# From the experts to the state-space stage: another order of tiles, convolutions and closing, and normalisations applied by ScalarE

## The reference

```python
x = x + _layernorm(attention(_layernorm(x)))      # over the 16 heads of each token
x = x + _layernorm(experts(_layernorm(x)))        # 16 routed experts of 64, top 4, and a shared one of 512
x = x + _layernorm(mamba_block(_layernorm(x)))    # two directions, 512 channels, 16 states
x = x + _layernorm(bitlinear(_layernorm(x)))      # 256 -> 1024 -> 256, relu squared
```

## Time and profile before

| | us |
|---|---|
| median of 3 runs (7385.79 to 7387.61) | 7387.34 |
| the profiled execution | 7389.32 |
| its span, first to last instruction | 7388.0 |
| TensorE busy | 5764.9 (78%) |
| VectorE busy | 5744.5 (78%) |
| GpSimd busy | 4502.9 (61%) |
| ScalarE busy | 3204.9 (43%) |

### The profile page before, as it was taken

The page is one execution under the profiler, slowest core; times in us unless marked ns, Lnnn a source line. Parts: engine busy times, 40 slices in busy tenths (PEclk is TensorE's granted clock), DMA queues, the critical chain, the costliest instruction groups (busy, mean ns, idle before and its releaser), DMA issues. The chain is left out here.

```text
span 7388.0 us, 59778 instructions
## 1 busy us (share of the span) xinstructions
PE 5764.9 (78%) x18532; PEld 3272.5 (44%) x18532; DVE 5744.5 (78%) x6592; ACT 3204.9 (43%) x6391; POOL 4502.9 (61%) x2698
## 2 busy tenths in 40 slices
PE   5778788787787877878778787787877878778887
PEld 4444354343553435534355343544435434454443
DVE  5589964899648995599964998649986599765997
ACT  1166511665116641266412664126641266313763
POOL 3179740897409964199641995419954299443994
PEclk8899998999899998999889998899988999889998
DMA  2011110111101111011110111101111011110111
GB/s 84 17 37 42 36 46 16 40 41 50 30 15 44 41 47 36 15 39 42 45 36 15 40 42 43 44 9 42 42 39 44 12 42 42 40 41 12 45 41 39
DMA packets 238118, 271.64 MB, mean 37 GB/s; under 512 B 144906, under 2 KB 194994, under 8 KB 231860
## 3 DMA queue, kind: packets, MB, share of 16 engines
q1 hardware_dynamic: 237748, 267.25, 11.2%
HBM read 246.13 MB, written 21.07 MB: 36 GB/s over the span
## 5 line engine op out<-in xcount | busy, mean ns | idle before, releaser
L1192 DVE TENSOR_TENSOR_SCAN wk<-ps,wk 128x1024 f32<-128x1024 f32 x1024 | 2316.3, 2275 | 105.4 <-POOL wk L1813 82.0
L1813 POOL TENSOR_TENSOR wk<-wk 128x1024 f32<-128x1024 f32 x1024 | 2380.3, 2360 | 9.2
L1683 ACT ACTIVATE ps<-wk,Aneg 128x255 f32<-128x255 f32 x4096 | 1704.1, 462 | 1218.1 <-DVE wk L1192 1183.8
L1407 PE MATMUL ps<-wk,ident 128*128 128x512 f32 x4096 | 2019.4, 618 | 24.1 <-DVE wk L1212 24.1
L431 POOL TENSOR_SCALAR rstd<-mv 128x4 f32<-128x4 f32 x146 | 36.0, 247 | 2293.4 <-DVE mv L424 2293.4
L1202 DVE TENSOR_TENSOR wk<-wk,ps 128x1024 f32<-128x1024 f32 x856 | 1021.6, 1193 | 14.4 <-PE ps L1402 8.7
L1407 PEld LDWEIGHTS ps<-wk,ident 128*128 128x128 f32 x4096 | 738.1, 197 | 631.7 <-issue 599.4
L1402 PE MATMUL ps<-wk,sel 112*128 112x256 bf16 x856 | 244.4, 286 | 853.1 <-DVE wk L1202 819.3
L537 POOL TENSOR_TENSOR wk<-wk 128x4096 f32<-128x4096 f32 x64 | 529.3, 8275 | 292.9 <-ACT wk L659 292.9
L1402 PEld LDWEIGHTS ps<-wk,sel 112*128 112x128 bf16 x856 | 84.1, 98 | 1153.9 <-DVE wk L1202 1018.1
L1353 PE MATMUL ps<-xnp,inT 128*128 128x256 f32 (+1 forms) x2048 | 561.6, 401 | 33.3 <-DVE wk L1168 13.7
(11 more groups left out here) (187 smaller groups left out, 8039.0 us busy)
## 6 DMA issues: line engine op xcount, KB each, us to landing
wk<-bc_scr SPq DMA_DIRECT2D x256, 512.0 KB, 3.6
wk<-bc_scr SPq DMA_DIRECT2D x56, 384.0 KB, 3.4
wk<-in_wgT SPq DMA_DIRECT2D x8, 1536.0 KB, 6.6
wk<-in_wuT SPq DMA_DIRECT2D x8, 1536.0 KB, 9.6
wk<-in_wdn SPq DMA_DIRECT2D x8, 1536.0 KB, 6.3
wk<-in_x SPq DMA_DIRECT2D x18, 512.0 KB, 4.0
o_scr<-wk SPq DMA_DIRECT2D x64, 128.0 KB, 3.0
wk<-o_scr SPq DMA_DIRECT2D x32, 256.0 KB, 3.4
```

Of the source, the lines that this page charges most:

```text
L1192: V.tensor_tensor_scan(h, in_time(d, flat(decay(m))), h, 0.0, ALU.mult, ALU.add).then_inc(scanned, 1)
L1407: mm = nc.tensor.matmul(bank(j), ident[:], h[:, 2 * j:2 * j + 2, :] .rearrange("p e t -> p (e t)"), start=first, stop=last)
L1683: nc.scalar.activation(decay(m)[:, e, rest(d)], dl[g % 2][:, e, rest(d)], ACT.Exp, scale=Aneg[:, d, e, n:n + 1]).then_inc(dA_done, 1)
L1813: nc.gpsimd.tensor_tensor(hb[n], du[g % 2], col(Bb[j % 2][:, n % NB, :]) .broadcast_to([P, NDI, MC]), ALU.mult).then_inc(dbu, 1)
```

## The change

`FIRST` becomes: X of unit 0, XD and LG of unit 0, X of unit 1. TensorE's order is X(0) four times, tile 4, XD, LG, LG, tile 5, two X(1), tile 6, two X(1), tile 7. The Z pieces of unit 0 become `GATE`, behind the first row of C, and their copies stand in unit 0 at states 0 to 3. VectorE convolves unit 0, does the softplus operation, then convolves unit 1, and takes the statistics of chunk 1's output before unit 0 and those of the residual sum behind state 1. ScalarE applies both normalisations of chunk 1 (`apply_close`), as an Identity activation with rstd for a scale and `shift` = -mean * rstd for a bias, ahead of the decays of states 0 and 4; GpSimd makes `shift` (`ln_shift`), adds the residual behind state product 1 and makes the second rstd and shift behind state product 2. The transposes of chunk 1 become pieces XE at states 4 to 7 of unit 0 and their copies stand at states 8 to 11; units 2 and 3 wait for them before their first X piece. Places in `wk` move so that `xc` no longer lies under `wdn`.

```diff
-        wdn = area(104 * KB, NJ, C)
+        wdn = area(101 * KB, NJ, C)
...
+        at = 113 * KB
+        inj = [area(at + i * DS * NDI, DS, NDI) for i in range(2)]
...
+        shift = area(at + 2 * MC + DS // 2 * NDI, NT // NCH)
...
+            XE_PE = {4: (0, 0), 5: (1, 0), 6: (0, 1), 7: (1, 1)}
+            XE_ACT = {8: (0, 0), 9: (1, 0), 10: (0, 1), 11: (1, 1)}
...
-            FIRST = (((X, 0, 0), (X, 0, 1)), ((X, 0, 2), (X, 0, 3)), ((X, 1, 0), (X, 1, 1)), ((X, 1, 2), (X, 1, 3)),
-                     ((XD, 0, 0),), ((Z, 0, 0), (Z, 0, 1)), ((LG, 0, 0),), ((LG, 0, 1),),
-                     ((Z, 0, 2), (Z, 0, 3)))
+            FIRST = [(X, 0, e) for e in range(NDI)] + [(XD, 0, 0), (LG, 0, 0), (LG, 0, 1)] + \
+                [(X, 1, e) for e in range(NDI)]
+            GATE = [(Z, 0, e) for e in range(NDI)]
...
-                    for g in range(2):
-                        for e in range(NDI):
-                            conv(g, e)
-                    ln_stats(dve, ecs, ytok, 1, 3, e_ev)
-                    ln_apply(dve, ecs, ytok, 1, 3)
-                    dve.wait_ge(e_added, NT)
-                    ln_stats(dve, ecs, xt, 1, 4)
-                    ln_apply(dve, ecs, xt, 1, 4)
+                    for e in range(NDI):
+                        conv(0, e)
                     softplus(0)
-
-                    dve.wait_ge(e_xn_ready, 3 * KC)
+                    for e in range(NDI):
+                        conv(1, e)
...
+                    ln_stats(dve, ecs, ytok, 1, 3, e_ev)
...
+                            if m == 1:
+                                dve.wait_ge(e_added, NT)
+                                ln_stats(dve, ecs, xt, 1, 4)
...
+                        if kind == X and i == 0 and g in (2, 3):
+                            pe.wait_ge(xe_ev, KC * (g - 1))
...
-                    for n, slot in enumerate(FIRST):
-                        for piece in slot:
+                    for piece in FIRST[0:NDI]:
+                        pre(piece)
+                    down(CT)
+                    for piece in FIRST[NDI:NDI + 3]:
+                        pre(piece)
+                    for n in range(2):
+                        down(CT + 1 + n)
+                        for piece in FIRST[NDI + 3 + 2 * n:NDI + 5 + 2 * n]:
                             pre(piece)
-                        if n < CT:
-                            down(CT + n)
+                    down(NT - 1)
...
-                    xn_tensor(pe, ecs, 1, 4, (0, 2))
-                    pe.wait_ge(e_xn_ready, 3 * KC)
...
                     weights(0)
+                    for piece in GATE:
+                        pre(piece)
...
+                    def apply_close(src, c, nth):
+
+                        act.wait_ge(xe_nb, 2 * (nth - 2))
+                        for i in range(CT):
+                            t = c * CT + i
+                            nc.scalar.activation(ytok[:, t, :], src[:, t, :], ACT.Identity, bias=shift[:, i:i + 1],
+                                                 scale=rstd[:, t:t + 1]).then_inc(ecs[4], 1)
...
+                        if g == 0 and n in XE_ACT:
+                            k, pair = XE_ACT[n]
+                            act.wait_ge(xe_mm, sorted(XE_ACT).index(n) + 1)
+                            at = CH + pair * MC
+                            nc.scalar.copy(xnT[:, k, at:at + MC], pre_slot((XE, k, pair))).then_inc(xe_ev, 1)
...
+                    silu_conv(0)
+                    experts_out(CT)
+                    pre(FIRST[NDI:NDI + 3])
+                    for what in ("abs", "exp"):
+                        soft(0, what)
+                    experts_out(CT + 1)
                     for what in ("ln", "less"):
                         soft(0, what)
-                    xn_scalar(act, ecs, 1, 2, (0, 2))
+                    experts_out(CT + 2)
+                    silu_conv(1)
+                    experts_out(CT + 3)
...
+                            if m == 0:
+                                apply_close(ytok, 1, 3)
+                            if m == 4:
+                                apply_close(xt, 1, 4)
...
+                    def ln_shift(c, nth):
+
+                        rs = rstd[:, c * CT:(c + 1) * CT]
+                        pool.wait_ge(ecs[2], 2 * (nth + 1))
+                        if nth > 3:
+                            pool.wait_ge(ecs[4], nth * CT)
+                        nc.gpsimd.tensor_tensor(shift, mv[:, c * CT:(c + 1) * CT, 0], rs, ALU.mult).then_inc(xe_nb, 1)
+                        pool.wait_ge(xe_nb, 2 * (nth - 3) + 1)
+                        nc.gpsimd.tensor_scalar(shift, shift, -1.0, None, ALU.mult).then_inc(xe_nb, 1)
...
-                    ln_rstd(pool, ecs, 1, 3)
-                    add_residual(pool, ecs, 1, 3)
-                    ln_rstd(pool, ecs, 1, 4)
                     part_c(0)
                     for what in ("lost", "delta", "du"):
                         softplus(0, what)
+                    ln_rstd(pool, ecs, 1, 3)
+                    ln_shift(1, 3)
                     pool.wait_ge(e_ev, NT)
...
+                            if m == 1:
+                                add_residual(pool, ecs, 1, 3)
+                            if m == 2:
+                                ln_rstd(pool, ecs, 1, 4)
+                                ln_shift(1, 4)
```

More of the change, by code:

```diff
@@ L171, in build @@
         hc = [area(at + NDI * MC * i, NDI, MC) for i in range(RC)]
-        inj = [area(at + NDI * MC * RC + i * DS * NDI, DS, NDI) for i in range(2)]
-        at += NDI * MC * RC + 2 * DS * NDI
+        at = 113 * KB
+        inj = [area(at + i * DS * NDI, DS, NDI) for i in range(2)]
+        at += 2 * DS * NDI
         xc = [area(at + i * MC // 2, MC, dt=BF16) for i in range(2)]
@@ L804, in batches @@
                 return NG4 * (g + 1) + max(g, 0)
-            X, Z, XD, LG, OUT, XN = "x", "z", "xd", "lg", "out", "xn"
+            X, Z, XD, LG, OUT, XN, XE = "x", "z", "xd", "lg", "out", "xn", "xe"
             AHEAD = {X: 2, XD: 1, LG: 1, Z: 1}
@@ L821, in pe_piece @@
                     return (XN,) + XN_PE[n]
+                if g == 0 and n in XE_PE:
+                    return (XE,) + XE_PE[n]
                 if n in PRE_PE:
@@ L826, in pe_piece @@
                 return None
-            FIRST = (((X, 0, 0), (X, 0, 1)), ((X, 0, 2), (X, 0, 3)), ((X, 1, 0), (X, 1, 1)), ((X, 1, 2), (X, 1, 3)),
-                     ((XD, 0, 0),), ((Z, 0, 0), (Z, 0, 1)), ((LG, 0, 0),), ((LG, 0, 1),),
-                     ((Z, 0, 2), (Z, 0, 3)))
-            FLAT = [p for slot in FIRST for p in slot]
-            NFIRST = len(FLAT)
-            SLOT = FLAT + [pe_piece(g, n) for g in range(NU) for n in range(DS) if pe_piece(g, n)]
+            FIRST = [(X, 0, e) for e in range(NDI)] + [(XD, 0, 0), (LG, 0, 0), (LG, 0, 1)] + \
+                [(X, 1, e) for e in range(NDI)]
+            GATE = [(Z, 0, e) for e in range(NDI)]
+            NFIRST = len(FIRST)
+            SLOT = FIRST + GATE + [pe_piece(g, n) for g in range(NU) for n in range(DS) if pe_piece(g, n)]
             AT = {p: m for m, p in enumerate(SLOT)}
@@ L856, in build @@
                 "sp_1 sp_ln sp_t sp_c sp_s sp_r sp_sum delta du_done dA_done dbu scanned inj_a inj_e inj_h injected zeroed c_bc "
[L857 removed]
+                "cm sig gated out_mm out_ev xn_mm xn_ev xe_mm xe_ev xe_nb c_part kept pw psig",
                 "x_in0 x_in1 wt_in h_mm relu_done sq_done f_mm f_ev",
@@ L1240, in square @@
                             .then_inc(sq_done, 1)
-                    for g in range(2):
-                        for e in range(NDI):
-                            conv(g, e)
-                    ln_stats(dve, ecs, ytok, 1, 3, e_ev)
-                    ln_apply(dve, ecs, ytok, 1, 3)
-                    dve.wait_ge(e_added, NT)
-                    ln_stats(dve, ecs, xt, 1, 4)
-                    ln_apply(dve, ecs, xt, 1, 4)
+                    for e in range(NDI):
+                        conv(0, e)
                     softplus(0)
-                    dve.wait_ge(e_xn_ready, 3 * KC)
-                    dve.wait_ge(pre_ev, len([p for p in FLAT if p in PLACE]))
+                    for e in range(NDI):
+                        conv(1, e)
+                    dve.wait_ge(pre_ev, len([p for p in FIRST if p in PLACE]))
+                    dve.wait_ge(conv_done, 2 * NDI)
                     for i in range(2):
@@ L1332, in take_slot @@
                             pe.wait_ge(xn_ev, AT[p] - AT[(XN,) + XN_PE[min(XN_PE)]] + 1)
+                        elif p[0] == XE:
+                            pe.wait_ge(xe_ev, AT[p] - AT[(XE,) + XE_PE[min(XE_PE)]] + 1)
                         elif p[0] == X:
@@ L1339, in pre @@
                         kind, g, i = piece
-                        if kind == XN:
+                        if kind in (XN, XE):
                             return ahead_t(piece)
@@ L1387, in ahead_t @@
                         kind, k, pair = piece
-                        pe.wait_ge(mcs[4], 3 * CT)
```

(10 more changed lines are left out.)

2 lines of the change are left out of this document (1 added, 1 removed).

## The result

The changed kernel takes 7332.28 us (median of 4 runs, 7330.87 to 7339.13), the kernel before on the same chip 7387.48 (4 runs, 7385.79 to 7387.96): ratio 0.9926, 95% interval 0.9911 to 0.9941. That is 55.2 us faster; 64 were forecast (7323), so nine did not come.

The account below looks back on a forecast made before the run. VectorE sets the pace in unit 0 (busy 65.19 of 66.81 us), so an earlier first scan carries through. 11.3 - 1.66 - 1.3 + 0.65 - 0.9 = 8.1 us per sequence, 65 in eight: 7323 us, range 7303 to 7356.

Parts of the forecast that it names:

- Passage: From the experts to the state-space stage: first scan at 408.7 instead of 420.0, 11.3 us gained per sequence.
- Statistics and the new wait: Unit 0: residual statistics on VectorE cost 1.66 us and the fourth scan waits 1.3 us for GpSimd, per sequence.
- TensorE's lateness: Unit 0, third weighing: VectorE's wait of 1.05 us for TensorE falls to 0.4, 0.65 us gained per sequence.
- XE: Unit 0, state 8: transpose copies make the convolution 1.9 us late, half comes back; net 0.9 lost (bounds 0.5, 1.9).
- (a): Before tile 4 and in unit 0: TensorE's clock falls in new gaps, half the gain eaten; 29 us gained, 7358; chance 0.14.
- (c): Output tiles run at 1.2 GHz, each costing 5.2 us more; slower, 7489 us with all four; chance 0.04.
- (b): Unit 0: GpSimd, not VectorE, sets the pace; 6.4 us gained per sequence, 51 us together, 7336; chance 0.10.
- (d): Before the first scan: the closing's hand-overs cost twice as much; 1.1 us left per sequence, 7378; chance 0.06.

Follow-up runs that it names:

- the run with the first scan first: Changed kernel with GpSimd making two state products before any closing step, closing steps later in unit 0, XE copies a state earlier: 7304.32 us, ratio 0.9888.

## Why the prediction was right, and where it was short

*Passage: right.* 10.91 for 11.3. Tile 7's copy starts 35.70 after the first X piece (35.5 forecast), Ln is over before tile 6 ends, the shift takes 0.53 (0.6), the four applications 2.08 (2.1). The table load starts 0.01 behind the last application, and from it to the decays is 1.30 again. So the drain of 1.38 that the Trainium skill states (ScalarE: Activation LUTs, What ACT_TABLE_LOAD costs) is not seen here either.

*Statistics and the new wait: right.* 1.60 for 1.66, 1.13 for 1.3. The second set of applications costs nothing by itself.

*TensorE's lateness: too small.* The wait at the third weighing and a small one behind it are gone wholly: 1.05 + 0.14 = 1.19, not 0.65.

*XE: the term that failed.* The step said "X starts at 457.4, the convolution 1.18 later (364.94 to 366.12), 458.6: 1.9 late. Half of it comes back". The lateness is right (1.80 for 1.9). But nothing came back: softplus took 3.14 for 2.27, so the term is 1.80 + 0.87 = 2.67, outside its own bounds of 0.5 and 1.9. The step took GpSimd's product as fixed by ScalarE's copies, as in the earlier trace rows. GpSimd had meanwhile lost ground on VectorE: its 16 state products end 39.3 us after the first scan (34.5 before), because it carries the sums (2.77), a wait of 2.92 for the statistics and rstd with shift (416.63 - 414.70 = 1.93) between them, 7.6 together, and starts them only 2.8 earlier against that scan. So its softplus product waits for no one but its own work, and starts 0.29 us before VectorE's operation. Three runs confirm it. With the second rstd later GpSimd's products end 2.8 earlier, and softplus takes 1.22. With the copies a state earlier 3.64 of unit 0 go, 3.54 of them the 2.67 and the 0.87 by which softplus (1.40) is shorter there than in the kernel before. With the closing in front of unit 0 GpSimd is early again, and the step comes out as forecast: X late by 1.80, softplus 1.22 for 2.27, net 0.75 for 0.9. So the lateness was priced rightly, and what failed is that the step left out the closing work that other steps of the same prediction had given GpSimd.

Sum: 10.91 - 1.60 - 1.13 + 1.19 - 2.67 = 6.70 by terms, 6.76 by scans; 8.1 was forecast. That is 10.7 less in eight sequences. TensorE's term covered 0.54 a sequence of a larger miss, and 1.7 of the span is the early start of the first passage, which is luck.

*The rivals.* (a) fell: the two gaps ahead of the X pieces are there (1.33 and 0.87), but the first tile starts as forecast and takes 5.34. Its last part, a late X piece of which nothing comes back, came true for another reason. (Its own time, 7358, lies outside the range that was said to hold most of it.) (c) fell with it. (b) fell: one scan inside unit 0 waits for GpSimd. (d) fell: the first scan is released by ScalarE, on time. What no rival named: a gain inside unit 0 can be taken back in later units. In the change as it stands that did not happen (units 1 to 7 unchanged), and this was luck of timing: in all seven variants with a shorter unit 0 later units were longer, by 1.7 to 5.0 us a sequence in the five without filler and by 0.4 to 2.1 in the two with it.

Open: what decides whether TensorE's clock outlives a given idle time. The runs show that the same 2.18 and 1.68 us can go either way, not why.

## What to carry to other kernels

Price a step that moves an operation by what it meets next on the other engine: where GpSimd's product started 0.29 and 0.57 us ahead of VectorE's softplus, that operation took 1.9 and 1.6 us longer. Work that one step of a forecast gives to an engine belongs in the times of every later step that waits for that engine or meets it. When an experiment shortens one stage as expected and the total stands still, compare the lengths of all later stages with the granted clock beside them, before dropping the theory. Where TensorE idles a little in each unit and its output is wanted soon after, filler that adds zero can bring back part of what an edit has won: 26 us in each of two kernels here, and nothing where the clock was up.

## What the hardware did that was not expected

Four of VectorE's scale-and-shift operations of 128x256 took 1.38 us with GpSimd idle and 9.39 beside its products, 2.35 each. GpSimd is shut out as well: the cast of 112x256 took 0.39 in the changed kernel, and 1.39 in the run with the first scan first, where it starts 1.4 us into the softplus operation:

```profile
441.52 1.39 POOL L1799 CAST wk<-wk 112x256 bf16<-112x256 f32 x1
```

With matmuls of zero weights in the idle time TensorE's granted clock was 1.00 from 543 to 558, and the output part behind them took 1.10; without them it was 0.89, and 1.76.
